# A differential-attention decoder layer on Trainium2: fetches of packed keys issued by ScalarE, those of packed queries by SyncE

## Time and profile before

| | |
|---|---|
| median of 3 runs | 619.63 us (618.93 to 621.52) |
| profiled execution, its own time | 615.97 us |
| its span | 614.7 us |
| PE busy | 555.1 us, 90% |
| DVE busy | 315.2 us, 51% |
| ACT busy | 221.7 us, 36% |
| POOL busy | 229.1 us, 37% |
| mean granted TensorE clock | 0.958 |
| DMAs with pack_q<-qk_parts, pack_k<-qk_parts | 48 and 48, 128 KB, 3.1 us median from issue to landing |
| SPq in the chain that ended last | 11% |

### The profile page before, as it was taken

One profiled execution on the slowest core, in us unless ns is written; L12 is line 12 of the kernel. 1 busy time (PEld: TensorE's weight loads), 2 busy tenths in 40 slices (PEclk: granted clock), 3 DMA queues, 4 the chain that ended last, 5 costly groups with the idle time before them and its releaser, 6 DMA issues.

```text
span 614.7 us, 10001 instructions
## 1 busy us (share of the span) xinstructions
PE 555.1 (90%) x3310; PEld 336.1 (55%) x3310; DVE 315.2 (51%) x681; ACT 221.7 (36%) x414; POOL 229.1 (37%) x473
## 2 busy tenths in 40 slices
PE   8967879899879877799999899997999999999998
PEld 6534336445546443575586456474666656666447
DVE  5749775597795995855242661111222222223282
ACT  7314544564554645615512200101333333333110
POOL 2534575455744554312010024562333333333100
PEclk9978979799998979899999999998999999999999
DMA  7651675232322138960039705222222232322731
GB/s 210 203 154 54 192 224 175 89 107 81 96 74 70 44 136 75 223 179 1 0 97 349 239 17 198 77 94 71 78 88 87 86 87 87 87 86 68 267 112 51
DMA packets 62192, 72.39 MB, mean 118 GB/s; under 512 B 14816, under 2 KB 55264, under 8 KB 60608
## 3 DMA queue, kind: packets, MB, share of 16 engines
q1 hardware_dynamic: 58352, 61.37, 35.5%
q0 software_dynamic: 3792, 10.39, 4.8%
HBM read 45.31 MB, written 26.03 MB: 116 GB/s over the span
## 4 chain that ended last, share of the span: by engine, by line
PE 35%; issue 19%; DMA 12%; SPq 11%; POOL 10%; DVE 9%; ACT 3%; POOLq 0%; DVEq 0%; ACTq 0%
PE ps L589 13%; DMA x_slots<-XN,slot_i 7%; POOL y_rows L1544 7%; PE ps L600 5%; SPq L1681 3%; SPq L1667 3%; PE ps L421 3%; SPq L1659 3%; PE ps L519 2%; DVE nmax L853 2%; DMA pack_k<-qk_parts 2%; PE ps L500 2%; SPq L1689 2%; PE ps L388 1%; POOL goes_to L1538 1%
## 5 line engine op out<-in xcount | busy, mean ns | idle before, releaser
L853 DVE TENSOR_REDUCE nmax<-ps 128x8 f32<-128x1024 f32 x64 | 77.8, 1217 | 41.5 <-PE ps L388 41.1
L644 PE MATMUL ps<-W,xt 128*128 x188 | 90.3, 603 | 1.2 <-ACT xt L1375 1.0
L1544 POOL DMA_INDIRECT y_rows<-yo,goes_to x47 | 45.8, 975 | 91.5 <-DVE yo L1086 91.5
L1279 ACT ACTIVATE prob<-ps 128x1024 f32<-128x1024 f32 x64 | 65.4, 1023 | 39.0 <-PE ps L409 39.0
L1079 DVE TENSOR_TENSOR sa<-sa,ps 128x256 f32<-128x256 f32 x47 | 19.8, 421 | 97.6 <-ACT sa L1382 97.6
L589 PE MATMUL ps<-xT,W1s 128*128 128x512 f32 x128 | 64.0, 624 | 2.4 <-ACT sil L1368 0.9
L589 PE MATMUL ps<-xT,W2s 128*128 128x512 f32 x128 | 60.9, 598 | 0.0
L600 PE MATMUL ps<-W3s,hTs 128*128 128x256 f32 x256 | 56.5, 381 | 3.5 <-DVE hTs L1012 3.5
L1368 ACT ACTIVATE sil<-ps 128x512 f32<-128x512 f32 x32 | 19.1, 597 | 106.8 <-PE ps L589 88.9
L1012 DVE TENSOR_TENSOR hTs<-sil,ps 128x512 f32<-128x512 f32 x32 | 22.0, 688 | 67.6 <-PE ps L589 63.5
L600 PEld LDWEIGHTS ps<-W3s,hTs 128*128 128x128 f32 x256 | 48.2, 190 | 13.2 <-DVE hTs L1012 5.1
(11 more groups left out here) (184 smaller groups left out, 877.0 us busy)
## 6 DMA issues: line engine op xcount, KB each, us to landing
W<-in_L_ffn_routed_w_dram SPq DMA_DIRECT2D x12, 1024.0 KB, 11.9
qk_parts<-part SPq DMA_DIRECT2D x28, 256.0 KB, 3.4
pack_q<-qk_parts SPq DMA_DIRECT2D x48, 128.0 KB, 3.1
pack_k<-qk_parts SPq DMA_DIRECT2D x48, 128.0 KB, 3.1
xg<-x_slots SPq DMA_DIRECT2D x47, 129.0 KB
x_slots<-zero SPq DMA_DIRECT2D x11, 512.0 KB, 11.1
yg<-y_rows SPq DMA_DIRECT2D x4, 1024.0 KB, 8.5
X<-in_x_dram SPq DMA_DIRECT2D x4, 512.0 KB, 7.6
```

Of the source, the lines that this page charges most:

```text
L644: r = t.matmul(ps[:, 2 + p, :], xt[:, p, k, :], W12[:, ds(e, 1), k, :].rearrange("p o f -> p (o f)"), start=(k == 0), stop=(k == KT - 1))
L853: v.tensor_reduce(nmax[:, s % 4, a, :, :], ps[:, b:b + 2, :].rearrange("p m (h t) -> p m h t", h=4), AX_X, ALU.max, negate=True).then_inc( ...
L1279: a.activation(prob[:, n:n + 2, :], ps[:, 2:4, :], ACT.Exp, scale=HD ** -0.5).then_inc(exped, 1)
L1544: g.indirect_dma_start(out=y_rows, out_offset=bass.IndirectOffsetOnAxis(ap=goes_to[:, n:n + 1].bitcast(U32), axis=0), in_=yo[:, p, :], in_ ...
```

## The change

ScalarE gets a function `fetch_keys(unit, n)`: it issues piece n of the keys of a unit (two DMAs), after the same two waits that SP makes. It is called first in ScalarE's `between`: for unit 2 at half-steps (1,1), (2,0) and (2,1), for the later units at (s,1) with s % 4 = 1, 2, 3, one piece each time, for s from 5 to 23. SP's `fetch` is called for the three pieces of queries only: of unit 2 all at s = 1, of a later unit one piece at each of s % 4 = 1, 2, 3. The count that TensorE waits for stays the same.

```diff
+UNIT_2_AT = ((1, 1), (2, 0), (2, 1))
...
+            def fetch_keys(unit, n):
+                u = unit % UNITS
+                if unit < UNITS:
+                    a.wait_ge(k_ones, unit + 1)
+                else:
+                    a.wait_ge(s_done, CS * (unit - UNITS + 1))
+                a.wait_ge(parts_stored[unit // 2], 16 * STORES)
+                for m in range(2):
+                    a.dma_start(Kp[u][MG * m + n:MG * m + KQ:3, :, :].rearrange("p h t -> p (h t)"),
+                                qk_parts[unit // 2, 2 + unit % 2, K_RUNS[n]:K_RUNS[n] + 2, :, m * HU:(m + 1) * HU, :].rearrange(
+                                    "q d h t -> (q d) (h t)")).then_inc(packed[u], 16)
...
             def between(s, a_):
+                if (s, a_) in UNIT_2_AT:
+                    fetch_keys(2, UNIT_2_AT.index((s, a_)))
+                if a_ == 1 and CB <= s and s // CB + UNITS - 1 < STEPS // CB and s % CB:
+                    fetch_keys(s // CB + UNITS - 1, s % CB - 1)
                 if (s, a_) == TURN_AT:
...
-                if s in (1, 2):
-                    fetch(2, range(3 * (s - 1), 3 * (s - 1) + 3))
+                if s == 1:
+                    fetch(2, range(len(Q_RUNS)))
                 if CB <= s and s // CB + UNITS - 1 < STEPS // CB and s % CB:
-                    fetch(s // CB + UNITS - 1, range(2 * (s % CB) - 2, 2 * (s % CB)))
+                    fetch(s // CB + UNITS - 1, range(s % CB - 1, s % CB))
```

## The result

The changed kernel takes 623.12 us (median of 20 runs, 618.77 to 625.52), the kernel before, run beside it, 618.49 us (20 runs, 615.83 to 621.52). The ratio is 1.0070, with a 95% interval of 1.0051 to 1.0089: by the ratio 4.3 us slower, where 2.7 us less was forecast.

The account below looks back on a forecast made before the run. The prediction took TensorE's waits for keys and maxima from SP's queue, with low clock behind them, as the bound, elsewhere TensorE or VectorE. 3.8 - 4.5 + 2.0 - 3.5 - 0.5 = -2.7 us gave 616.9 us; range 611.8 to 623.5.

Parts of the forecast that it names:

- first place, carried into step 9: From half-step (1,1) into step 9: ScalarE's wait for stores, low clock and step 6 together +3.8 us, bounds 0 and +5.
- unit 3: At 107.7 us: the wait of 2.82 us becomes 0.3 and the low clock goes, -4.5 us, bounds 0 and -5.6.
- ScalarE in the other places: Uncovered issues: +1.0 at (17,1), +0.6 at (19,1), +0.4 at (9,1) and (11,1); sum +2.0 us, between 0 and +8.
- unit 6: At 180.2 us: the wait of 1.70 us and 3.1 us of low clock go, -3.5 us, between 0 and -4.8.
- unit 7 and the end: Unit 7 at 206.4 us: -0.5 us, between 0 and -0.5.
- The first wait: Half-step (1,1): ScalarE stands for chunk 1's stores until 68.7 us, delaying exp(2,0) and making exps(2,1) 3.0 us late.
- the term of the low clock: Steps 2 and 3, behind the first idle stretch of 3 us: +1.5 us, between 0 and 2.5.
- Step 6: The 3.27 us wait for put_max shrinks, but VectorE's maxima of (8,1) are late next, so removing it gives nothing.
- 0, if the clock stays high: Lower bound of the +3.8 us into step 9: TensorE's clock stays high in both places and the old low stretch goes.
- Rival 2: ScalarE becomes the bound at all 18 places, above all (1,1): +4.5 us in sum, 624.1 us; chance 0.20.
- Rival 3: Waits for units 3 and 6 stay, since transfers, not issues, take the time: +4.3 us, 623.9 us; chance 0.10.
- Rival 1: The first wait, at (1,1), costs nothing: first term +0.8 instead of +3.8, sum -5.7 us, 613.9 us; chance 0.20.

Follow-up runs that it names:

- unit 2 alone: Kernel before with only unit 2's keys moved to ScalarE at (1,1), (2,0), (2,1), units 3 to 7 still fetched by SyncE: ratio 1.0112.
- the filler: Changed kernel plus 20 transposes with unused results on TensorE at the end of half-step (2,0), where it stands for exp(2,0): ratio 1.0045 to the kernel before.
- the cut lift: Changed kernel with unit 2 on SyncE, chunk 2's stores at s = 4, and VectorE's lift of the queries in three parts: ratio 0.9961 to the kernel before.
- the two runs with units 3 to 7 on SyncE: Kernel before with only unit 2's keys moved to ScalarE, 1.0112; kernel before with only a wait for chunk 1's stores added on ScalarE at (1,1), 1.0038.
- the stores later: Changed kernel with unit 2's keys back on SyncE and chunk 2's seven stores issued at s = 4, behind put_max(6): ratio 0.9962 to the kernel before.
- unit 2 on SyncE: Changed kernel with unit 2's keys fetched by SyncE again, keys of units 3 to 7 staying on ScalarE: ratio 0.9993 to the kernel before.

## Why the prediction was wrong

Point by point, counted in the profile of the changed kernel from (2,0) on, behind the 1.3 us that are not the change's:

| step | forecast | measured |
|---|---|---|
| first place, carried into step 9 | +3.8 | 7.08 - 1.31 = +5.8 |
| unit 3 | -4.5 | 3.22 - 7.08 = -3.9 |
| ScalarE in the other places, (10,0) to (18,1) | +2.0 | 4.43 - 3.22 = +1.2 |
| unit 6 | -3.5 | 4.41 - 4.43 = 0.0 |
| unit 7 and the end | -0.5 | 3.41 - 4.41 = -1.0 |
| sum | -2.7 | +2.1 |

- *The first wait* was right in place and size: exps(2,1) +2.7 us here, +3.2 with unit 2 alone and +3.3 with the filler, against 3.0. What was mis-sized is the term of the low clock: 1.5 us taken, 2.53 measured from (2,1) to (3,1) here (1.97 with unit 2 alone, nothing with the filler). The stretch behind the wait holds a projection of 1.98 us that takes 3.78. I had the bound of 2.5 and took less, though behind the three long waits before all matmuls were slow (0.61 us for eight, not 0.40).
- *Step 6* came as forecast: put_max(6) no longer late, VectorE's maxima late instead, shown by the cut lift. The old low clock came back behind this wait, and 0.6 us more were lost (6.50 to 7.08) where 0.7 was to come back (3.0 + 1.5 against 3.8); "0, if the clock stays high" did not occur. With the clock term this makes +5.8.
- *Unit 3* was right: 0.49 us of wait, clock 1.00, 3.9 us for 4.5.
- *The other places*: +0.95 at (17,1) for 1.0 forecast, nothing at (19,1) for 0.6. The other 0.3 up to (11,0) stands in the two runs with units 3 to 7 on SyncE as well (6.04 to 6.30, 3.00 to 3.25), so it is not ScalarE's.
- *Unit 6 failed.* The step that failed is "the wait of 1.70 us goes, and 3.1 us of low clock". I compared the landing of the keys with TensorE only, and not with the other thing that scores(24,0) waits for, VectorE's maxima of (23,1) (in the code its wait for `maxed` stands beside the one for `packed[u]`). The timeline of VectorE before had it:

```profile
179.91 1.23 DVE L853 TENSOR_REDUCE nmax<-ps 128x8 f32<-128x1024 f32 x1
181.06 0.17 DVE L992 RECIPROCAL den<-den 128x4 f32<-128x4 f32 x1
```

  It ended at 181.1 us, 0.8 before the keys. So of 1.70 us only 0.8 could go, 0.9 remained (1.07 measured), and the clock fell at the same place; 0.69 us for the next maxima took back what was left. The timeline of VectorE after; the first line ends at 187.75, and scores(24,0) runs at 187.90 us:

```profile
186.53 1.22 DVE L854 TENSOR_REDUCE nmax<-ps 128x8 f32<-128x1024 f32 x1
187.67 0.17 DVE L993 RECIPROCAL den<-den 128x4 f32<-128x4 f32 x1
```

  With the stores later the clock stayed up behind the same 1.07 us, and scores(24,1) waited 1.52 us instead; from (18,1) to (22,0) that gave 0.4 us, not 3.5. The wait of one instruction for two things was booked on the later one alone. At step 6 I had asked that question, here I had not.
- *Unit 7 and the end*: the wait of 0.50 us is gone, but the 1.0 us cannot be put down to it: with unit 2 alone, where SyncE fetches unit 7, the same stretch gave 0.9 (6.50 to 5.56).

The timed 623.1 us lies near the sums of rivals 2 and 3 (624.1 and 623.9), but by luck, since their mechanisms did not make it. Rival 2 is out: an issue on ScalarE takes 0.59 us, 0.57 and 0.86 where SyncE issues six queries beside it. That pair took 1.46 us, in the filler run as well, against 1.13 alone; with twice SyncE's row it would have been 2.5. SyncE's six took 4.10 and 3.74 us in these two, 3.95 in the kernel before and 4.75 with unit 2 on SyncE, so on that side nothing is to be seen. The Trainium skill, "Perfetto Trace Analysis", section "DMA Instruction — HWDGE (DVE, Sync)", has the block that makes the descriptors locked for exclusive use. The 0.3 us more may be that lock; no run shows that it is. Rival 3 holds in part: the last DMA to land is now a query's, and the wait for it was 0.49 to 1.03 us in six profiles with these keys first and 2.40 in the seventh, the filler's. Rival 1 did not occur. What failed in the sum is thus first unit 6 (3.5 us) and then the first place with its low clock (2.0 us). The sum of the measured terms, +2.1, still lies under the 4.3 us (3.2 to 5.5) of the timed runs. The two halves of the change, timed alone, give 1.0112 and 0.9993, which agree with 1.0070 within their intervals. How much of the rest is low clock that falls in more executions than in the one profiled, no run settles.

## What to carry to other kernels

Before a DMA is handed to a compute engine, look at what its wait needs at that moment: the queue that had the DMA came late to the wait, the new one comes early, and all its arithmetic stands behind it. Move only what finds its semaphore passed, and look what small, urgent transfer it will go out beside. For each wait that is to go, read when the same instruction's other inputs were ready; only the difference is to be had, and the low clock need not go with it (here it went where 0.49 us of the wait remained, and came back where 1.07 did).

## What was not expected of the hardware

- An issue on ScalarE's queue runs beside the activation sent before it: 1.13 us of two issues at 73.15 beside an exp of 1.02 us at 73.07.
- A transfer of 6 KB took 5.43 and 4.97 us to land while six of 128 KB went out from another queue, and 1.94 and 1.95 us at the same place without them.
- A stand of 1.07 us had the same low clock behind it (0.50 from 188.0 to 194.5 us) as one of 1.70 us; in the profile with the stores later the same stand of 1.07 us left it at 0.99 (181.6 to 184.3 us). Which it will be, no row here tells beforehand.
